# Inverse roots by Newton's method on VectorE, a contraction interleaved with steps, and first weights prepared alone

## What is computed

```python
# layer 0
z_norm = layer_norm(z, ln_w, ln_b)                    # over the 64 channels
a = (z_norm @ W_ap + b_ap) * sigmoid(z_norm @ W_ag + b_ag) * m
b = (z_norm @ W_bp + b_bp) * sigmoid(z_norm @ W_bg + b_bg) * m
z = z + einsum('bikc,bkjc->bijc', a, b) @ W_z + b_z
# layer 1
x = layernorm(z, ln1_w, ln1_b)
left, right = sigmoid(x @ left1) * (x @ left2), sigmoid(x @ right1) * (x @ right2)
p = layernorm(einsum('nsre,nkre->nske', left, right), ln2_w, ln2_b)
out = z + (p @ out_w) * sigmoid(x @ gate)
```

## Time and profile before

| | us |
|---|---|
| span of the profiled execution | 1036.7 |
| that execution's own time | 1038.49 |
| median of three runs | 1036.89 |
| TensorE busy | 832.8 (80%) |
| VectorE (DVE) busy | 763.3 (74%) |
| ScalarE (ACT) busy | 635.2 (61%) |
| GpSimd (POOL) busy | 587.9 (57%) |
| mean granted TensorE clock | 0.953 of full speed |

### The profile page before, as it was taken

One profiled execution on the slowest core, in us unless ns is written; L12 is line 12 of the kernel. 1 busy time (PEld: TensorE's weight loads), 2 busy tenths in 40 slices (PEclk: granted clock), 3 DMA queues, 4 the chain that ended last, 5 costly groups with the idle time before them and its releaser, 6 DMA issues.

```text
span 1036.7 us, 26385 instructions
## 1 busy us (share of the span) xinstructions
PE 832.8 (80%) x9820; PEld 794.4 (77%) x9820; DVE 763.3 (74%) x1851; ACT 635.2 (61%) x866; POOL 587.9 (57%) x409
## 2 busy tenths in 40 slices
...
GB/s 81 92 164 162 155 206 263 325 333 263 231 271 298 270 42 238 315 219 274 237 249 108 112 207 257 298 279 131 299 265 122 151 303 252 257 248 235 196 227 191
DMA packets 173238, 228.72 MB, mean 221 GB/s; under 512 B 11064, under 2 KB 109624, under 8 KB 171064
## 3 DMA queue, kind: packets, MB, share of 16 engines
...
...
## 4 chain that ended last, share of the span: by engine, by line
PE 40%; DVE 21%; DMA 16%; issue 12%; ACT 4%; POOL 4%; SPq 3%; DVEq 0%; POOLq 0%; ACTq 0%
PE bank L1052 16%; PE bank L1032 7%; DVE stats L895 6%; DMA xin<-in_x_dram 6%; PE bank L1033 6%; PE ps_w L1082 5%; DVE split L939 4%; DMA chunk<-xcol 3%; DMA chunk<-xt 2%; DVE xc L932 2%; PE ps_t L1067 2%; DVE var L902 2%; DMA xt<-xt 2%; POOL rstd L633 2%; DVE xc L924 2%
## 5 line engine op out<-in xcount | busy, mean ns | idle before, releaser
L633 POOL TENSOR_TENSOR rstd<-var,minus_half 128x8 f32<-128x8 f32 x192 | 341.2, 1778 | 388.2 <-DVE var L902 388.2
L1052 PE MATMUL bank<-rhs,lhs 128*128 128x128 f32 x2048 | 246.7, 281 | 17.0 <-DVE lhs L875 9.2
L1052 PEld LDWEIGHTS bank<-rhs,lhs 128*128 128x128 f32 x2048 | 238.0, 196 | 20.6 <-DVE lhs L875 8.9
L689 ACT ACTIVATE sig<-bank 128x512 f32<-128x512 f32 x256 | 151.6, 601 | 72.2 <-PE bank L1033 69.3
L716 ACT ACTIVATE xt<-ps_x 128x1024 bf16<-128x1024 bf16 x128 | 130.9, 1023 | 61.9 <-PE ps_x L1093 45.9
L1093 PE MATMUL ps_x<-ident_b,split 128*128 128x128 bf16 x1024 | 85.6, 232 | 90.1 <-DVE split L939 89.6
L932 DVE TENSOR_TENSOR xc<-xc,rstd 128x504 f32<-128x504 f32 (+1 forms) x192 | 139.2, 725 | 23.0 <-POOL xc L647 19.8
L1093 PEld LDWEIGHTS ps_x<-ident_b,split 128*128 128x128 bf16 x1024 | 67.1, 103 | 103.0 <-DVE split L939 102.1
L1032 PE MATMUL bank<-w_rhs,chunk 128*128 128x128 bf16 x1024 | 135.2, 227 | 8.2 <-DVE rhs L867 3.3
L1032 PE MATMUL bank<-w_lhs,chunk 128*128 128x128 bf16 x928 | 131.4, 234 | 6.7 <-DVE lhs L867 4.4
L1082 PE MATMUL ps_w<-w_out,opair 128*128 128x128 f32 x896 | 124.2, 283 | 13.4 <-ACT opair L708 13.0
...
## 6 DMA issues: line engine op xcount, KB each, us to landing
...
xin<-in_x_dram SPq DMA_DIRECT2D x128, 256.0 KB, 4.5
...
```

The lines of the kernel that those rows point to most:

```text
L633: g.tensor_tensor(rstd[:, m % 2], var[:, m % 2], minus_half[:, :], ALU.pow).then_inc(rooted, 1)
L689: a.activation(sig[:, s], v[:, 0:C, :], ACT.Sigmoid).then_inc(gated, 1)
L1052: last = mm(bank[:, n], operand["lhs"][:, kh, c, :], operand["rhs"][:, kh, c, :], start=kh == 0, stop=kh == HALVES - 1)
```

## The change

Five things are changed.

1. **Roots.** GpSimd's power function is gone. VectorE works out the inverse root of two steps at once, in nine instructions of 128 x 16 (`root`, n = 0 to 8): -variance/2, a first guess from the bits of the number, and two rounds of Newton's method. Each waits for the one before it. `root_in_gap()` puts one of them behind nearly every other instruction of VectorE, also between the four statistics instructions. The nine take the place of two `var` instructions.
2. **Centre and norm.** GpSimd centres all z and x steps, and now multiplies by the root (`normalise`) in z steps 0 to 19 and in all x and p steps; VectorE keeps that for z steps 20 to 63, where the root lies in PSUM (`ps_w`). The lags of z, x and p steps grow by one to three ticks.
3. **Masks.** GpSimd's masks of contraction 0 come one in each tick from tick 22 to 69; of contractions 1 and 2 GpSimd masks the other half of the operand.
4. **Contraction 3** has the x steps of quadrant 6 (before "x alone") in its ticks. Its result goes to the lower half of `lhs` instead of `quad`, and layer 1's operand half goes to `quad`.
5. **Start.** Four loads of x, then the six loads that the first weights need; the others follow at ticks 1 and 3 or are issued by ScalarE. The first weights are prepared in ticks 1 and 2, the others in ticks 7 to 9.

The core of the diff:

```diff
+GUESS = float(0x5f375a86 - (1 << 30) - (1 << 22))
+ROOT_FACTOR = 1.5 * ROOT_C
+I32 = mybir.dt.int32
...
-Z_LAGS = dict(load=-2, stats=0, variance=0, root=0, centre=1, norm=1, high=1, low=2, turn_x=2, xt=3,
-              col=3, store=4, project=3, gates=4, make=5)
-X_LAGS = dict(turn=0, turn_out=0, mix=1, load=1, add=2, keep=3, stats=3, variance=3, root=3, centre=4,
-              norm=4, high=4, low=5, turn_x=6, xt=6, store=7, project=0, gates=0, make=1)
-P_LAGS = dict(stats=-1, variance=-1, root=-1, centre=-1, norm=0, turn=0, turn_out=1, mix=1, spread=-2,
-              gate=0, gate_out=2, scale=2, load=2, residual=3, store=4, gate_load=-4, project=0, gates=1, make=1)
-LATE_Z_LAGS = dict(Z_LAGS, turn_x=3, xt=4, col=4, store=5)
+Z_LAGS = dict(load=-2, stats=0, centre=1, norm=2, high=2, low=3, turn_x=3, xt=4,
+              col=4, store=5, project=4, gates=5, make=6)
+X_LAGS = dict(turn=0, turn_out=0, mix=1, load=1, add=2, keep=3, stats=3, centre=5,
+              norm=5, high=5, low=6, turn_x=7, xt=7, store=8, project=0, gates=0, make=1)
+P_LAGS = dict(stats=-2, centre=0, norm=1, turn=1, turn_out=2, mix=2, spread=-1,
+              gate=1, gate_out=3, scale=3, load=3, residual=4, store=5, gate_load=-3, project=0, gates=1, make=1)
+LATE_Z_LAGS = dict(Z_LAGS, turn_x=4, xt=5, col=5, store=6)
...
-        tick("second half", {2: Z_LATE - 2, 5: Z_LATE - 1}.get(i), [48 + 2 * i, 49 + 2 * i], spill=(0, 0, i // 2 - 1) if i in (3, 5, 7) else None)
-    contraction(0, dict(zip((0, 1, 3, 4, 6, 7, 9, 10), range(Z_LATE, 4 * STEPS))),
-                {0: (0, 0, 3), 3: (0, 1, 0), 7: (0, 1, 1), 11: (0, 1, 2), 15: (0, 1, 3)})
+        tick("second half", {3: Z_LATE - 2, 4: Z_LATE - 1}.get(i), [48 + 2 * i, 49 + 2 * i], spill=(0, 0, 0) if i == 6 else None)
+    contraction(0, dict(zip((0, 1, 2, 3, 5, 6, 8, 9), range(Z_LATE, 4 * STEPS))),
+                {2: (0, 0, 1), 4: (0, 1, 0), 6: (0, 0, 2), 8: (0, 1, 1), 10: (0, 0, 3), 12: (0, 1, 2), 15: (0, 1, 3)})
...
-        tick("x alone", X_BASE + 2 * STEPS + n)
-    contraction(3)
+        tick("x in contraction", X_BASE + 2 * STEPS + n, unit=(3, n))
...
-Z_EARLY, Z_LATE = 22, 56
+Z_LATE = 56
+NORM_EARLY, NORM_LATE = 20, 4 * STEPS
+OTHERS_AT = 7
...
+def first_masks_at(t):
+    return range(max(0, t - MASK_FIRST), min(FIRST_MASKS, t - MASK_FIRST + 1))
...
+VECTOR_MASKS = {0: "lhs", 1: "lhs", 2: "rhs"}
...
-    return m < Z_EARLY or Z_LATE <= m < P_BASE
-CENTRED = []
+    return m < P_BASE
+def norm_on_pool(m):
+    return m < NORM_EARLY or m >= NORM_LATE
...
+        def roots_of(pair):
+            if OTHERS_AT + 5 <= 2 * pair and not norm_on_pool(2 * pair):
+                return ps_w[:, pair % 2, 0:2 * COLS].rearrange("p (s t) -> p s t", s=2)
+            return rstd[:, pair % 2]
+        def root_of(m):
+            return roots_of(m // 2)[:, m % 2]
...
+            for m in range(RING):
                 load_x(m)
-            for dst, src in loads:
-                sp.dma_start(dst, src).then_inc(loaded, 16)
-            sp.wait_ge(zeroed, 1)
-            for dst, src in loads_diag:
-                sp.dma_start(dst, src).then_inc(loaded, 16)
+            for dst, src in first_loads:
+                sp.dma_start(dst, src).then_inc(first_loaded, 16)
             for t in range(T_END):
                 for m in due("load", t):
-                    if m >= 2:
+                    if m >= RING:
                         load_x(m)
+                if t == 1:
+                    for dst, src in loads:
+                        sp.dma_start(dst, src).then_inc(loaded, 16)
...
-            def root(m):
-                pool.wait_ge(normed, after(m - 2))
-                pool.wait_ge(var_done, after(m))
-                g.tensor_tensor(rstd[:, m % 2], var[:, m % 2], minus_half[:, :], ALU.pow
-                                ).then_inc(rooted, 1)
+            def mask_later(q, u):
+                op = VECTOR_MASKS[q]
+                table, half = (mask_ki, P * (q == 1)) if op == "lhs" else (mask_kj, P)
+                if u == 0:
+                    pool.wait_ge(made, after(2 * (NEEDS[q] - GROUPS) - 1))
+                part = operand[op][:, 0, CG // 2 * u:CG // 2 * (u + 1), :]
+                g.tensor_tensor(part, part, table[:, 0, half:half + P].unsqueeze(1).broadcast_to(
+                    [P, CG // 2, P]), ALU.mult).then_inc(masked_p, 1)
             def centre(m):
-                kind, _, _, c0 = step(m)
                 h = m % 2
                 pool.wait_ge(stats_done, after(m))
-                pool.wait_ge(normed, after(m - 1))
-                if m - 2 >= P_BASE:
-                    pool.wait_ge(turned, after(m - X_BASE - 2))
-                else:
-                    pool.wait_ge(low_done, after(m - 2))
-                src, lo = (quad[:, c0:c0 + COLS, :], 0) if kind == "p" else (xin[:, m % RING], 1)
-                g.tensor_tensor(xc[:, h, :, lo:], src[:, :, lo:],
-                                stats[:, h, :, 1:2].broadcast_to([P, COLS, C - lo]),
+                pool.wait_ge(low_done, after(m - 2))
+                g.tensor_tensor(xc[:, h, :, 1:], xin[:, m % RING, :, 1:],
+                                stats[:, m % 4, :, 1:2].broadcast_to([P, COLS, C - 1]),
                                 ALU.subtract).then_inc(centred_p, 1)
+            def normalise(m):
+                h, lo = m % 2, 0 if m >= P_BASE else 1
+                pool.wait_ge(*centred_by(m))
+                pool.wait_ge(rooted, after(m // 2))
+                g.tensor_tensor(xc[:, h, :, lo:], xc[:, h, :, lo:],
+                                root_of(m).unsqueeze(2).broadcast_to([P, COLS, C - lo]),
+                                ALU.mult).then_inc(normed_p, 1)
...
+                for n in first_masks_at(t):
+                    mask_operand(n)
+                for m in due("centre", t, "zx"):
+                    centre(m)
                 for m in due("residual", t):
                     add_residual(m)
-                for n in pool_masks_at(t):
-                    if t < MASK_TWO:
-                        pool.wait_ge(normed, after(t - 2))
-                    mask_operand(n)
-                for m in due("root", t):
-                    root(m)
+                for m in due("norm", t):
+                    if norm_on_pool(m):
+                        normalise(m)
+                for q, u in later_masks_at(t):
+                    mask_later(q, u)
...
+                    last = v.bn_stats(stats[:, m % 4, c:c + 2, :].rearrange("p a s -> p (a s)"), src)
+                    if c == COLS - 2:
+                        last.then_inc(stats_done, 1)
+                    root_in_gap()
+            unfinished = []
+            def root(pair, n):
+                before = 8 * pair
+                if n == 0:
+                    dve.wait_ge(rooted, after(pair - 1))
+                    dve.wait_ge(stats_done, after(2 * pair + 1))
+                    v.tensor_scalar(minus_var[:, :, :], stats[:, 2 * (pair % 2):2 * (pair % 2) + 2, :, 2],
+                                    C * EPS, -0.5, ALU.add, ALU.mult).then_inc(newton, 1)
+                if n == 1:
+                    dve.wait_ge(newton, before + 1)
+                    v.tensor_scalar(guess[:, :, :].bitcast(I32), minus_var[:, :, :].bitcast(I32),
+                                    -0.5, GUESS, ALU.mult, ALU.add).then_inc(newton, 1)
+                if n in (2, 6):
+                    dve.wait_ge(newton, before + n)
+                    v.tensor_tensor(term[:, :, :], guess[:, :, :], guess[:, :, :], ALU.mult).then_inc(newton, 1)
+                if n == 3:
+                    dve.wait_ge(newton, before + 3)
+                    v.tensor_tensor(term[:, :, :], term[:, :, :], minus_var[:, :, :], ALU.mult).then_inc(newton, 1)
+                if n == 4:
+                    dve.wait_ge(newton, before + 4)
+                    v.scalar_tensor_tensor(term[:, :, :], term[:, :, :], 5 / 3, term[:, :, :], ALU.add, ALU.mult
+                                           ).then_inc(newton, 1)
+                if n == 5:
+                    dve.wait_ge(newton, before + 5)
+                    v.scalar_tensor_tensor(guess[:, :, :], term[:, :, :], 1.25, guess[:, :, :], ALU.add, ALU.mult
+                                           ).then_inc(newton, 1)
+                if n == 7:
+                    dve.wait_ge(newton, before + 7)
+                    v.scalar_tensor_tensor(term[:, :, :], term[:, :, :], 2.25, minus_var[:, :, :], ALU.mult, ALU.mult
+                                           ).then_inc(newton, 1)
+                if n == 8:
+                    dve.wait_ge(newton, before + 8)
+                    dve.wait_ge(*normed_by(2 * pair - 3))
+                    v.scalar_tensor_tensor(roots_of(pair), term[:, :, :], 1.5, guess[:, :, :], ALU.add, ALU.mult
+                                           ).then_inc(rooted, 1)
+            def root_in_gap():
+                if unfinished:
+                    pair, n = unfinished.pop()
+                    root(pair, n)
```

(53 more changed lines are left out.)

343 lines of the change are left out of this document (199 added, 144 removed).

## The result

The changed kernel takes 1076.3 us (median of four runs, 1075.0 to 1077.7) against 1036.7 of before: a ratio of 1.038 [1.034, 1.043]. It is slower by 39.6 us, where +13 was forecast; 1076.3 lies above the stated range of 1005 to 1068. The span of the profiled execution went from 1036.7 to 1076.1 us.

What follows compares the result with a forecast made beforehand. VectorE and GpSimd were taken to set the pace in the z steps, TensorE from 288 us on. Terms -1 + 25 - 8 + 2 - 17 + 1 + 4 + 7 = +13 on 1036.9 gave 1050 us; 8-in-10 range 1005 to 1068.

Steps and rivals of the forecast that it cites:

- The exclusion: A VectorE instruction with all inputs in SBUF and a whole-tile GpSimd instruction exclude each other, in turns.
- the largest term: Z steps 20 to 53: +25 us, at 4.3 us per step with exclusion.
- the second half: Second half and contraction 0: -8 us from 83, ends -14 and 0.
- the x and p steps with chunks: X with chunks, twice: +2 us; p with chunks, twice: +4; TensorE covers VectorE's waits.
- Root instructions mostly miss GpSimd's spans: Rival, whole kernel: short root instructions settle where they fit, z steps 3.45 us; -43, some 995 us; chance 0.23.
- half the waits: Rival, whole kernel: z steps and early ticks 3.9 us; about -13 to -5, some 1028 us; chance 0.20.
- Slower z steps leave no backlog: Second half and contraction 0: a reason given, with earlier x loads and later spills, for the -8 us.
- The 42 us for the contraction: Second half: contraction 0 taken as about 42 us, after eight ticks of about 4.
- waits reach TensorE: Rival, x and p ticks: late makes delay projections; 1068 us; chance 0.15 together with contraction 3 not overlapping (1067).
- P alone: Last p steps: +7 us, 3.6 us a step against 3.11 before, ends -2 and +12.
- Contraction 3: Contraction 3 among its x steps: -17 us, TensorE bounds the merged stage; ends -12 and -19.
- Start: Start and z steps to 20: -1 us, step 4's load by 14.5 us, step 20 at 86.5 against 87.7.

Runs made afterwards that it cites:

- psum_roots: The changed kernel with minus_var and half of the root's term values in PSUM in z steps 12 to 63, products reordered; 1041.3 us, 1.007 of before.
- short_roots: The changed kernel with three of the nine root instructions (n0, n1 and n8), output not the reference's; 1007.3 us, 0.973 of before.
- c3_and_start: The kernel before with contraction 3 among its steps and the change's start, roots still on GpSimd; 1001.7 us, 0.971 of before.
- no_p_norm: The changed kernel without GpSimd's multiplication by the root in p steps; 1060.0 us, 1.024 of before.
- root_block: The changed kernel with all nine root instructions of a pair in one block behind the odd step's statistics; 1133.7 us, 1.096 of before.

## Why the prediction was wrong

The exclusion was right and so was the largest term. What failed is two steps of the sum: the second half, put at -8 for a backlog that would be gone, measured +3.3; and the x and p steps with chunks, put at +6 because TensorE would cover VectorE's waits, measured +24.1. Together they are 29 us off, and the other terms come out 3 us below their forecast. In us, on the profiled executions:

| stretch | forecast | measured |
|---|---|---|
| start, to step 20 | -1 | -4.2 (87.7 to 83.5) |
| steps 20 to 53 | +25 | +23.0 (117.3 to 140.2) |
| steps 53 to 64, with contraction 0 | -8 | +3.3 (91.7 to 95.1) |
| steps 64 to 96, with contractions 1 and 2 | +2 | +13.3 (205.3 to 218.7) |
| steps 96 to 112, contraction 3 | -17 | -19.3 (84.9 to 65.6) |
| steps 112 to 128 | +1 | +2.7 |
| steps 128 to 160, p with chunks | +4 | +10.8 (208.3 to 219.1) |
| steps 160 to 176 | 0 | -0.6 |
| from step 176 on | +7 | +10.4 (60.7 to 71.1) |
| sum | +13 | +39.4 |

**Exclusion, worked: right.** 4.25 us per z step, forecast 4.3, in turns of 4.76 and 3.71 us from low to low where the working had 4.8 and 3.8, and the turns in the timeline are those of the working (n0 behind the mask, n3 behind the centre, n4 behind the next mask). "Root instructions mostly miss GpSimd's spans" and "half the waits" fell with it. One slip in the working changes nothing: 33 steps of 3.3 us are 109, not 112. The scalings n0 and n1 do wait when they write to SBUF (0.95 and, at 1057.03 us, 0.48). The Trainium skill ("SBUF — State Buffer", "Who interferes with whom") allows a scaling to contend only in a two-port mode, and says that an instruction with at most one SBUF input outside these modes does not. psum_roots agrees with both: with one side in PSUM the same scaling took 0.18 us inside a mask. That it is the two-port mode is the page's reason; no run here separates the mode from the place.

**The second half: the step that failed first.** "Slower z steps leave no backlog" was to give 8 us. There was none to win: steps 53 to 64 took 92.7 us in psum_roots and 90.9 in short_roots, with z steps much quicker than in the changed kernel (95.1), and 89.9 in c3_and_start. TensorE's waits in that stretch of the kernel before (205 to 297 us) are for low (7.1 us), masks (6.5) and makes (6.5), none for a transfer. The change keeps the waits for VectorE (makes 7.6, masks 7.1, low 3.1) and adds one for GpSimd's mask (2.4); without GpSimd's masks the stretch takes 90.3. The 42 us for the contraction had no row behind it: it took 46, as before.

**X and p with chunks: TensorE does not cover VectorE's waits.** I had this as a rival at 0.15 together with another; it is what happened, with 24 us where the forecast had 6. My own working had 5.2 and 4.4 us of VectorE in even and odd ticks against 4.8 a tick before, and took the mean of them, as if a short tick paid for a long one. TensorE's waits for VectorE's makes and masks in the x steps with contractions 1 and 2 (318 to 537 us of the changed kernel; who waited for whom, us, times, longest):

```profile
PE bank L1223 <- DVE rhs L971: 4.8, 3, 2.4
PE bank L1223 <- DVE lhs L971: 4.6, 3, 2.4
PE bank L1204 <- DVE rhs L963: 4.0, 9, 1.1
...
PE bank L1204 <- DVE lhs L963: 2.4, 4, 0.9
```

That is 9.4 us for masks and 6.4 for makes. Before, it was 5.4 and 0.2. With three root instructions instead of nine it is 9.0 and 2.4, and steps 64 to 96 take 209.0 us instead of 218.7: the six that are left out carry 9.7 of the 13.3. The rest lies with the split of the masks, the lags or the other three; no run separates these. Part of this I had not costed at all: the change gives half of the masks of contractions 1 and 2 to GpSimd. Here is that half, and VectorE's, which lie beside it:

```profile
L706 POOL TENSOR_TENSOR lhs<-lhs,masks x16: 1260/1710/1794, 357.5 to 409.7; 128x512 f32<-128x512 f32 x16
```

```profile
L971 DVE TENSOR_TENSOR lhs<-lhs,masks x16: 678/1516/1757, 376.3 to 412.5; 128x512 f32<-128x512 f32 x16
```

VectorE's mask of half a unit takes 1.52 us in the median where alone it takes 0.68. Before, it did a whole unit in 1.26 us. VectorE has half the work and the same time (19.3 us, 19.4 before), and the low of these steps went from 10.9 to 16.1 us. In the p steps with chunks the makes come late behind root instructions (726 to 946 us):

```profile
PE bank L1204 <- DVE rhs L963: 12.4, 9, 3.6
PE bank L1204 <- DVE quad L963: 8.3, 6, 3.6
PE bank L1204 <- DVE lhs L963: 4.8, 5, 1.8
```

25.5 us, against 5.0 before on the same lines. With three root instructions instead of nine it is 8.4, and steps 128 to 160 take 203.8 us instead of 219.1. The exclusion is at work here too: the 144 root instructions of these steps take 49.6 us, where 0.16 each would be 23. The stretch is only 10.8 longer than before; 9.8 us of other waits of TensorE (5.6 for the norm, 4.2 for ScalarE) have shrunk to 0.7. Covered work is covered only if it is done before the engine that covers it needs it; a mean per tick says nothing of that.

**P alone: the right step, the end forgotten.** Steps at 3.36 us against 3.11, less than the 3.6 forecast (+3.7). But from step 191 on 20.8 us instead of 14.1: the last root is uncovered and its instructions wait in turn for the residual of GpSimd (timeline of VectorE, two of them):

```profile
1058.03 1.24 DVE L1014 TENSOR_TENSOR term<-guess 128x16 f32<-128x16 f32 x1
...
1061.47 1.25 DVE L1024 SCALAR_TENSOR_TENSOR guess<-term,guess 128x16 f32<-128x16 f32 x1
```

That the rest of the 6.7 is the longer lags of the last steps is only argued: no_p_norm keeps 19.3 us there.

**Contraction 3: right** (-19.3; undone alone it costs 24 us of its stretch, done alone it gives 1.5% of the time). **Start: right in sign, and hidden.** The early weights bring step 4 from 36.4 to 15.6 us; by step 20 only 4 of these 21 us are left. From step 4 to 20 before took 51.3 us, c3_and_start 57.3 (the other weights are prepared there) and the changed kernel 67.9: 10.6 for roots on VectorE and what came with them. With roots on GpSimd 15 us stay (72.4 against 87.7).

So of +39 the other two parts are about -30 (c3_and_start, 0.971 of before) and the roots on VectorE, with the norms, masks and lags that were moved for them, about +70. The price of the rival "waits reach TensorE" was nearly right in the sum, by luck: it added 3 us to each stage with chunks and 6 to "x every other tick", 18 in all; measured against the forecast it is 18 (2 to 6 a stage, which with its contraction got 4 to 7 us longer) and 2. What lifts the time above its 1068 is the second half.

## What to carry to other kernels

Count, for each small VectorE instruction that you add, where its operands lie. With two inputs in SBUF, or a scaling from SBUF to SBUF, it costs up to the whole of the GpSimd instruction that it meets, so nine of them are not nine times 0.1 us. One operand in PSUM takes that away: before you leave a small chain to GpSimd, try its temporaries in PSUM (in the z steps 109.6 us, against 117.3 and 113.1 with GpSimd's root and VectorE's centre). Moving part of an elementwise job from VectorE to GpSimd so that both work on it at once gained nothing here, since both read two operands from SBUF. And where the covering engine waits for its turn in a queue, ask for the latest instruction before the one that it needs, not for the mean load of the tick.

## What the runs showed of the chip beside

- The exclusion lasts for the whole instruction and works in turns: of two back-to-back GpSimd instructions, a waiting 16-element VectorE instruction gets in between them and ends some 0.03 us behind the first.
- A VectorE instruction that depends on the one before it follows it by 0.21 us (root_block); when independent work stands between, a root instruction takes the queue 0.08 us (149.80 to 149.87).
- A GpSimd instruction can lose as well: its half-unit masks take 1.71 us in the median beside VectorE's (1.26 at the shortest).
- GpSimd's power function (128x8, L633 of the kernel before, 1.78 us in the mean) holds nothing up: 197 of VectorE's whole-tile instructions with two SBUF inputs lie wholly inside one, and none of them took over 0.70 us. So the root that the change took from GpSimd was the one instruction there that did not exclude VectorE.
